# An attention layer with a mixture-of-experts layer on one core: two orders of work in the shared steps, and a split of the last products

## The reference, cut to what matters

```python
x = x + attention(layernorm(x))                  # q, k, v, elu + 1, cumsum(phi_k * v) * phi_q, Wo
h = layernorm(x).reshape(2048, 256)
logits = h @ router_w                            # 8 experts
top_logits, top_indices = top_k(logits, 2)
scores = softmax(top_logits)
combined = sum over the two chosen e of  scores * ((silu(h @ w1g[e]) * (h @ w1u[e])) @ w2[e])
shared = (silu(h @ w_gate) * (h @ w_up)) @ w_down
return x + combined + shared
```

## Time and profile before

| what | value |
|---|---|
| runs | 359.17 us median of 3 (358.69 to 359.64) |
| the profiled execution | 358.56 us |
| its span, first to last instruction | 356.6 us |
| granted TensorE clock, mean | 0.996 of full speed |
| TensorE busy | 340.7 us |
| VectorE busy | 236.7 us |
| ScalarE busy | 215.4 us |
| GpSimd busy | 193.9 us |

### The profile page before, as it was taken

How to read it: one execution, slowest core, us unless ns; L and a number is a source line. 1 busy time by engine, 2 the same in 40 slices (tenths; PEclk the granted TensorE clock), 3 DMA queues, 4 the chain that set the end, 5 groups by cost and what they waited for, 6 DMA issues and landing times.

```text
span 356.6 us, 9230 instructions
## 1 busy us (share of the span) xinstructions
PE 340.7 (96%) x2971; PEld 256.8 (72%) x2971; DVE 236.7 (66%) x587; ACT 215.4 (60%) x391; POOL 193.9 (54%) x282
## 2 busy tenths in 40 slices
PE   7998989999899899999999999999999999999993
PEld 7877868888787798898988565555656556666652
DVE  4988899899788788787788555453544544334441
ACT  3669858787695877955636255454445554554451
POOL 4778986676783647647043543454353435443335
PEclk9999999999999999999999999999999999999998
DMA  7986242556673465545786444758486776766660
GB/s 189 385 213 143 95 121 45 137 136 193 148 219 81 123 209 118 110 145 171 235 254 154 107 72 80 110 74 116 65 117 85 104 98 83 107 101 94 91 71 9
DMA packets 77469, 46.43 MB, mean 130 GB/s; under 512 B 61041, under 2 KB 72561, under 8 KB 77041
## 3 DMA queue, kind: packets, MB, share of 16 engines
q1 hardware_dynamic: 63088, 35.08, 39.5%
q0 software_dynamic: 9664, 10.71, 19.0%
q10 hardware_dynamic: 4672, 0.07, 0.9%
HBM read 19.09 MB, written 12.97 MB: 90 GB/s over the span
## 4 chain that ended last, share of the span: by engine, by line
PE 68%; DVE 14%; ACT 6%; issue 6%; POOL 3%; DMA 2%; SPq 0%; DVEq 0%; POOLq 0%; ACTq 0%
PE bU L1064 13%; PE bG L1064 13%; PE bV L1087 7%; PE bQ L1087 6%; PE bG L238 6%; PE bD L941 6%; PE bU L238 6%; PE bV L238 3%; PE bK L238 3%; PE bK L1044 2%; DVE ab L1542 2%; PE bT L941 2%; PE bQ L238 1%; DVE st L1419 1%; ACT xn L1162 1%
## 5 line engine op out<-in xcount | busy, mean ns | idle before, releaser
L1542 DVE SCALAR_TENSOR_TENSOR ab<-bU,sg 128x512 f32<-128x512 f32 x64 | 44.1, 689 | 69.5 <-PE bU L1064 53.1
L772 POOL DMA_INDIRECT out_y<-xs,dst_row x32 | 49.7, 1552 | 60.9 <-DMA out_y<-xs,dst_row 33.9
L1202 ACT ACTIVATE sg<-bG 128x512 f32<-128x512 f32 x64 | 37.9, 593 | 41.0 <-PE bG L1064 27.1
L1064 PE MATMUL bG<-we,work 128*128 (+1 forms) x216 | 52.6, 380 | 0.0
L1064 PE MATMUL bU<-we,work 128*128 (+1 forms) x216 | 52.6, 379 | 0.0
L571 POOL DMA_INDIRECT x_rows<-rows,slot_u x32 | 40.2, 1257 | 20.5 <-DVE slot_u L1593 10.7
L1369 ACT ACTIVATE ws_h<-ab 128x512 f16<-128x512 f32 x36 | 22.7, 630 | 41.5 <-DVE ab L1542 41.5
L1860 DVE TENSOR_TENSOR ws_h<-ab,ws_h 128x512 f16<-128x512 f32 x36 | 24.9, 692 | 20.8 <-ACT ws_h L1369 20.8
L1209 ACT ACTIVATE ah<-ab 128x512 f16<-128x512 f32 x32 | 20.1, 629 | 26.6 <-DVE ab L1542 26.4
L1064 PEld LDWEIGHTS bG<-we,work 128*128 128x128 f16 (+1 forms) x216 | 20.7, 99 | 19.3 <-issue 1.6
L1064 PEld LDWEIGHTS bU<-we,work 128*128 128x128 f16 (+1 forms) x216 | 19.8, 99 | 17.3
(11 more groups left out here) (327 smaller groups left out, 822.0 us busy)
## 6 DMA issues: line engine op xcount, KB each, us to landing
stage<-in_w_expert SPq DMA_DIRECT2D x24, 512.0 KB, 4.7
we<-in_w_shared SPq DMA_DIRECT2D x3, 1024.0 KB, 11.9
xs<-bo POOLq DMA_DIRECT2D x8, 256.0 KB, 4.3
out_y<-xs SPq DMA_DIRECT2D x8, 256.0 KB, 3.0
xs<-in_x SPq DMA_DIRECT2D x1, 1280.0 KB, 18.5
x_rows<-we SPq DMA_DIRECT2D x9, 134.0 KB
xs<-in_x SPq DMA_DIRECT2D x3, 256.0 KB, 3.9
work<-x_rows SPq DMA_TRANSPOSE x40, 3.3
```

The costliest lines, as they stand in the source:

```text
L772: pool.indirect_dma_start(out_rows, bass.IndirectOffsetOnAxis(ap=dst_row[:, b:b + 1], axis=0), ya[b % NY], None, bounds_check=NT * P - 1, ...
L1064: ins = pe.matmul(dst[t * n:(t + 1) * n, :], x2[:, hi * KC + k, t * n:(t + 1) * n], w[t][lo][:, k, half, :], start=s == 0 and k == 0, stop ...
L1202: act.activation(sg[q][:], src[:], ACT.Silu, scale=1.0 / WS).then_inc(S["sg_done"], 1)
L1542: dve.scalar_tensor_tensor(out=ab[q][:], in0=src[:], scalar=1.0 / WS, in1=sg[q][:], op0=ALU.mult, op1=ALU.mult).then_inc(S["a_done"], 1)
```

## The change

Four orders are changed. In steps 4 to 7 GpSimd does `gaps(i - 1)` right behind `norm1(i + 1)`, ahead of `add_bo` and `token_ids`. In the same steps ScalarE does the third `silu` of the step ahead of the step's third `expert_hi`. In `scatter`, the wait for the destinations stands ahead of the wait for the result. `expert_down` can run some of its three products of halves: the first two of block 34 are put ahead of the last block's turns, the third stays behind them.

```diff
             for i in range(4, B):
                 if i < B - 1:
                     norm1(i + 1)
+                gaps(i - 1)
+                if i < B - 1:
                     add_bo(i + 1)
                 token_ids(i)
-                gaps(i - 1)
                 norm2(i)
...
+                pool.wait_ge(S["dst_done"], b + 1)
                 pool.wait_ge(S["y_done"], b + 1)
-                pool.wait_ge(S["dst_done"], b + 1)
...
-            def expert_down(b):
+            def expert_down(b, parts=range(3)):
...
                 for s, (a, lo) in enumerate(((aT_h[n], 0), (aT_h[n], 1), (aT_l[n], 0))):
+                    if s not in parts:
+                        continue
...
-                ins.then_inc(S["o_ps"], 1)
+                if 2 in parts:
+                    ins.then_inc(S["o_ps"], 1)
...
+            expert_down(NBLK - 2, (0, 1))
             turn_high(NBLK - 1)
             pe.wait_ge(S["al_done"], NP * B + NBLK)
...
             ins.then_inc(S["tl_ps"], 1)
-            expert_down(NBLK - 2)
+            expert_down(NBLK - 2, (2,))
             expert_down(NBLK - 1)
...
                 expert_hi(part_of_step(i, first + 1))
                 choice(i - 1)
+                silu(n + 2, 0)
                 expert_hi(part_of_step(i, first + 2))
-                silu(n + 2, 0)
                 act_hi(j, 2)
```

## The result

The changed kernel takes 355.64 us (median of 4 runs, 355.24 to 356.11), the kernel before 358.93 (4 runs, 358.59 to 359.64). The ratio is 0.9906, 95% interval 0.9884 to 0.9929: 3.3 us faster, beyond the bound of 0.3%. The forecast was 3.0 less, 356.1.

What follows compares the result with a forecast made beforehand. TensorE, busy 340.7 us, was taken as the bound, so only its idle time or the tail counts. 1.52 + 1.52 + 0.1 - 0.1 + 0 + 0 = 3.0 off 359.17 gave a median of 356.1; range 354.8 to 357.3.

Steps and rivals of the forecast that it cites:

- ahead of 88.6: GpSimd, steps 4 to 7: in its new place dlog was taken to end under 88.6, within bounds of 86.8 and 91.4.
- The terms of 1.52: TensorE's waits for silu ahead of bG in steps 4 and 5: each vanishes whole, 1.52 us apiece.
- Step 6's 0.1: TensorE's small stall in step 6: twelve matmuls that take 1.31 show 1.41, so 0.1 us is gained.
- cover: ScalarE's silu ahead of the expert part: adds nothing once dlog is early, about 1.0 us per stall if dlog stays late.
- The late load: Load for ScalarE's fourth expert part, step 4: costs 0 to 0.5, taken as 0.1; as rival 2.2, chance 0.11.
- transposes that don't move: Step 4: the fourth expert part's load is issued at 93.2 behind these, so it does not come earlier.
- The tail: Last scatters: the last waits for the landing of block 33's scatter and stays 4.7 behind it; the split gains 0.
- 1.0 by spans: Last scatters: counted by the DMA spans alone, the split would end the kernel 1.0 us sooner; rival, chance 0.15.
- The swapped waits: The two waits of scatter: swapping them was taken as 0, bounds minus 0.1 to plus 0.1 at the end.
- dlog is still held: Rival, GpSimd: VectorE holds dlog to 91.4 in the new place, only silu's move gains, 1.0 twice: 357.2; chance 0.05.

Runs made afterwards that it cites:

- the late result: The changed kernel with ScalarE's result of block 33 put behind the last block's turn: 357.48 against 359.31 for the kernel before, ratio 0.9946.

## Why the prediction was right, and where not

**The place and the mechanism held.** dlog was held and not long by itself: 0.20 in the new place, ahead of 88.6, the bias load where it was, no idle time ahead of tanh in steps 4 to 6, no wait of TensorE for silu. GpSimd's order alone gives 0.9900, so that move is the cause. silu is 1.21 early (forecast 1.1).

**The stalls were undersized.** The terms of 1.52 measured 1.69 and 1.67 (step 5: 2.98 from bD to bG before, 114.00 to 116.98; 1.31 after, 112.97 to 114.28), since idle time in the rows begins at a modelled end that lies some 0.17 behind the point where the next product could have started. That is 0.32 that the sum lacked. Step 6's 0.1 measured 0.08.

**silu's move is cover**, as forecast: nothing on top (0.9900 without it), 0.95 per stall where dlog stays late (forecast 1.0). Without it the cover was 0.27 in step 4 (forecast 0.06). In step 7 silu waits 1.47 for TensorE and the part runs behind it, at no cost that the traces show.

**The late load didn't come.** The fourth part of step 4 starts without idle time ahead of it: 0 in place of 0.1. What came late was another thing, which the forecast had passed over with "Everything that comes after 93.44 in the step hangs on TensorE and moves ahead by 1.52 with it" and "In step 5 the pattern repeats": the transposes for step 6 hang on VectorE's queue and moved by one stall only, and 0.24 was lost in the profiled run. That the forecast saw "transposes that don't move" in step 4 and did not ask the same in step 5 is the wait that it missed. That they move by one stall only is shown; what makes them late enough to cost 0.24 stays open.

**The tail stayed**, for the reason given: the last scatter waits for the landing of block 33's, 4.72 behind it (before 4.69), with block 34's out 0.9 sooner; 1.0 by spans fell in two runs (the split alone 0.9997, the late result 5.00 in place of 3.8). The swapped waits were measured only together with the split: 0 for both.

**The sum as measured**: 1.69 + 1.67 + 0.08 - 0.24 = 3.20, against 3.0 forecast and 3.29 by the medians. That the forecast of 3.0 came so near is in part luck: the two omissions, 0.32 and 0.24, are of opposite sign. The place of the gain, two whole stalls, is not.

**A rival's ground.** For "dlog is still held" the forecast weighed the Trainium skill, SBUF — State Buffer, section "Who interferes with whom", and read from it a wait of one operation at most. The order with dlog behind the load has a row of 1.57, over the end of one operation and the whole of the next; counted from the end of the bias load ahead of it (112.55) it is one operation, so this run doesn't contradict that reading. In the new place this didn't matter, as dlog ended 1.8 ahead of the bias load. The other rule of the Trainium skill, Perfetto Trace Analysis, "DMA Instruction — SWDGE (GPSIMD)", that such a DMA's span ends with its descriptors and not with its data, is borne out by the tail: the span of block 33's scatter ends at 347.71, its traffic starts after 348.2.

## What to carry to other kernels

Where a tiny operation on GpSimd has a row many times its usual length that ends with a VectorE operation, move it to where its input becomes ready, not merely a few instructions up: here its row was 0.20 ahead of the queue's wait for ScalarE, and up to 1.77 behind it. Before reading such a row as time held, look whether the operation ahead of it on GpSimd is still in its own row. Price a stall of TensorE by the distance between the starts of products, not by the idle time in the row, and then ask of each DMA that feeds the next product which engine releases it and whether that engine moves as far. At the end of a kernel, look for the last thing that must have landed before shortening the work ahead of it: here the split freed 0.9 that the landing of an earlier scatter took back.

## What was not expected of the hardware

- In the changed kernel the last few dozen packets of two transposes moved only after a 16 KB packet of the instruction queue had ended, some 0.6 us behind the rest. In seven of eight runs with a loss TensorE began 1.44 to 1.49 behind that packet's end. That the packet held them is not shown by an edit.
- The 128x2 subtraction on GpSimd has a row of 0.19 to 0.20 where its input is all that it waits for, and of 0.75, 1.57 and 1.77 behind the bias load, each time ending 0.03 to 0.05 after a VectorE operation. Part of each long row lies under GpSimd's own work ahead of it, 0.45, 0.46 and 0.51.
- From the end of a scatter's traffic to the next register write behind its wait it took 0.4, and 1.0 more to the start of the DMA that waited, before the change and after.
